# Experts over lists of token rows, in blocks of 128 with register-addressed weights, in place of every expert over every token

## The reference

```python
x = x + attention(layernorm(x), ctx)          # 16 heads, causal, gate, Wo
xf = layernorm(x)
scores = softmax(xf @ gate_w)                 # 8 experts
top_scores, top_idx = top_k(scores, 2)
scale = zeros((T, E)).at[arange(T)[:, None], top_idx].set(top_scores)
xs = scale.T[:, :, None] * xf[None]           # an expert that was not chosen sees zeros
h = silu(einsum('etd,edh->eth', xs, w1)) * einsum('etd,edh->eth', xs, w3)
x = x + einsum('eth,ehd->etd', h, w2).sum(0)
```

## Time and profile before

| | |
|---|---|
| median of 3 runs | 680.01 us (677.1 to 682.3) |
| span of the profiled execution | 676.9 us |
| TensorE busy | 644.6 us, 95% |
| VectorE, ScalarE, GpSimd busy | 471.3, 379.5, 230.4 us |
| instructions | 13559 |

### The profile page before, as it was taken

One profiled execution on the slowest core, in us unless ns is written; L12 is line 12 of the kernel. 1 busy time (PEld: TensorE's weight loads), 2 busy tenths in 40 slices (PEclk: granted clock), 3 DMA queues, 4 the chain that ended last, 5 costly groups with the idle time before them and its releaser, 6 DMA issues.

```text
span 676.9 us, 13559 instructions
## 1 busy us (share of the span) xinstructions
PE 644.6 (95%) x5320; PEld 393.0 (58%) x5320; DVE 471.3 (70%) x981; ACT 379.5 (56%) x778; POOL 230.4 (34%) x283
## 2 busy tenths in 40 slices
PE   7887999999999999999999999999999999979997
PEld 3363565555565545554565556455456766768885
DVE  6637779998989999999989987412205533676454
ACT  2221456766646676667646677877784565123332
POOL 5005212522123115021005033385434434536662
PEclk9878799999999999999999899999999999999999
DMA  6985982010260000010093010102101021104100
GB/s 170 234 133 115 138 144 31 2 22 24 69 68 1 3 1 3 1 65 2 14 161 109 2 34 3 35 2 78 32 32 32 17 63 49 31 16 109 48 32 31
DMA packets 29305, 36.58 MB, mean 54 GB/s; under 512 B 5833, under 2 KB 16457, under 8 KB 29242
## 3 DMA queue, kind: packets, MB, share of 16 engines
q1 hardware_dynamic: 26248, 34.53, 24.6%
q10 hardware_dynamic: 946, 0.92, 0.4%
q0 software_dynamic: 2048, 0.27, 0.3%
HBM read 25.58 MB, written 8.06 MB: 50 GB/s over the span
## 4 chain that ended last, share of the span: by engine, by line
PE 45%; DVE 12%; ACT 3%; POOL 2%; issue 1%; DVEq 0%; ACTq 0%; POOLq 0%
PE bank L1600 9%; DVE pmax L1303 9%; PE bank L1578 8%; PE bank L1664 4%; PE bank L1666 4%; PE bank L1665 4%; PE bank L1429 3%; PE bank L1545 3%; PE bank L1685 2%; PE bank L1686 2%; ACT probs L1160 2%; PE bank L1688 2%; DVE xn_sb L1274 1%; PE bank L1610 1%; PE bank L1583 1%
## 5 line engine op out<-in xcount | busy, mean ns | idle before, releaser
L1160 ACT ACTIVATE probs<-bank 128x512 f32<-128x512 f32 (+4 forms) x592 | 283.2, 555 | 147.0 <-PE bank L1578 87.5
L1303 DVE TENSOR_REDUCE pmax<-bank 128x1 f32<-128x512 f32 (+6 forms) x640 | 322.7, 574 | 29.4 <-PE bank L1549 15.9
L1578 PE MATMUL bank<-qaug,kaug 64*128 64x512 f32 (+4 forms) x592 | 151.6, 455 | 2.5 <-DVE pmax L1303 1.1
L1600 PE MATMUL bank<-probs,vaug 128*32 128x256 f32 (+4 forms) x2048 | 142.3, 390 | 2.2 <-ACT probs L1160 1.8
L1545 PE MATMUL bank<-kaug,qaug 62*128 62x512 f32 (+6 forms) x640 | 135.0, 404 | 9.8 <-DVE stage L807 3.4
L1578 PEld LDWEIGHTS bank<-qaug,kaug 64*128 64x128 f32 (+1 forms) x592 | 66.2, 183 | 85.7 <-ACT probs L1160 29.8
L1545 PEld LDWEIGHTS bank<-kaug,qaug 62*128 62x128 f32 x640 | 76.5, 189 | 40.7 <-DVE pmax L1303 21.0
L1600 PEld LDWEIGHTS bank<-probs,vaug 128*32 128x32 f32 (+1 forms) x2048 | 52.3, 109 | 53.3 <-ACT probs L1160 18.4
L1032 POOL TENSOR_TENSOR h_lo<-v_sb,h_hi 128x512 fp32r<-128x512 f32 x31 | 40.1, 1295 | 66.3 <-ACT h_hi L1216 66.3
L1396 DVE SCALAR_TENSOR_TENSOR v_sb<-t_sb,v_sb 128x512 f32<-128x512 f32 x32 | 24.2, 757 | 45.2 <-POOL v_sb L1028 38.2
L1216 ACT ACTIVATE h_hi<-v_sb 128x512 fp32r<-128x512 f32 x32 | 20.4, 637 | 57.4 <-DVE v_sb L1396 55.5
(11 more groups left out here) (143 smaller groups left out, 824.4 us busy)
## 6 DMA issues: line engine op xcount, KB each, us to landing
qaug<-s_dram SPq DMA_DIRECT2D x32, 256.0 KB, 3.4
qaug<-q_parts SPq DMA_DIRECT2D x18, 256.0 KB, 9.2
q_parts<-stage SPq DMA_DIRECT2D x7, 512.0 KB, 2.9
k_parts<-stage SPq DMA_DIRECT2D x4, 512.0 KB, 5.0
w_sb<-in_w SPq DMA_DIRECT2D x4, 512.0 KB, 10.0
out<-x_sb SPq DMA_DIRECT2D x8, 256.0 KB, 2.3
ctx_sb<-in_ctx_t SPq DMA_DIRECT2D x3, 512.0 KB, 6.4
x_sb<-in_x SPq DMA_DIRECT2D x3, 512.0 KB, 6.3
```

Of the source, the lines that this page charges most:

```text
L1160: act.activation(probs[0:rows, u % NSLOT, h, off:CH], bank_of(e)[0:rows, off:CH], ACT.Exp, scale=DK ** -0.5).then_inc(act_read, 1)
L1303: dve.tensor_reduce(pmax[:, n % 2, qt, h, slot:slot + 1], bank[:, 0:w], AX_X, ALU.max).then_inc(dve_read, 1)
L1578: last.append(pe.matmul(pair[side][0][0:r, off:CH], keys_at(b, ROWS, hp, P * j, r), qaug[b:b + ROWS, p % 2, hp, off:CH], start=True, stop= ...
L1600: last = pe.matmul(psum[O_BANK][32 * h:32 * h + 32, q0:q1], vaug[0:r, col:col + 32], probs[0:r, u % NSLOT, h, q0:q1], start=(j == 0), stop ...
```

## The change

The feed's 32 dense steps go. In their place each token's row (scaled by its score) is written once for each of its two experts into a list in DRAM, and the lists are worked off in blocks of 128 rows. The lists are made twice: chunks 1, 2 and 3 together (`SETS[0]`), which give at most 24 blocks filled and 7 more for parts of blocks, 31, and chunk 0 (`SETS[1]`), which gives 15: 46 blocks, always run, empty ones on zeros. After `rank` of a chunk, `cnt` counts on TensorE and VectorE the rows ahead of each token and gives its two places (`slots`), `wide` makes the two scaled rows (GpSimd for chunks 1 and 2, VectorE for 3 and 0), and `scat` sends them by 8 indirect transfers from GpSimd's queue. After a set's last chunk, `tail` writes zeros behind each list (9 transfers by SP, 8 of them with an address that SP loads into a register), and `table` computes on VectorE which expert and which place each block has, and where each token's two results will lie.

A block i is then: `bl` (SP loads a register, then the rows), `bx` (2 transposes; ScalarE `row_hi`, VectorE `row_lo`), `bab` (6 products of 256 columns, w1 and w3 side by side; tanh on ScalarE, two VectorE instructions), `bh` (1 transpose; `h_hi`, `h_lo`), `by` (3 products of 256 columns, copied by ScalarE) and `bst` (SP stores 128 KB). The rows are now the stationary operand and the weights the moving one, at an address from a register that TensorE loads for each block. `back` fetches each token's two results by indirect transfers (4 for 256 tokens, in GpSimd's queue), `add` adds them and `out` stores.

```diff
-Y_BANKS = (5, 6)
+SETS = ((1, 2, 3), (0,))
+LAGS = {"bx": 0, "bab": 1, "bh": 2, "by": 3}
+RING = 3
+SET_OF = {c: s for s, chunks in enumerate(SETS) for c in chunks}
+ROOM = tuple(TPC * len(chunks) + 1 for chunks in SETS)
+COUNT = tuple(2 * TPC * len(chunks) + E - 1 for chunks in SETS)
+BLOCKS = [(s, b) for s, count in enumerate(COUNT) for b in range(count)]
+LAST_BLOCK = tuple(sum(COUNT[:s + 1]) - 1 for s in range(len(SETS)))
...
+XIN, YOUT, GOT = 4, 3, 3
+W_STEP = 3 * D
...
+            ("rank", c), ("cnt", c), ("wide", c), ("scat", c)] + ([("tail", SET_OF[c]), ("table", SET_OF[c])] if c == SETS[SET_OF[c]][-1] else [])
...
+def block_steps():
+
+    steps, count = [], len(BLOCKS)
+    for i in range(count + max(LAGS.values())):
+        for kind, lag in LAGS.items():
+            if 0 <= i - lag < count:
+                steps.append((kind, i - lag))
     return steps
```

The transfers of SP and GpSimd:

```diff
+                elif kind == "tail":
+
+                    s = e[1]
+                    sp.wait_ge(tail_ready, s + 1)
+                    sp.wait_ge(none_set, 1)
+                    sp.dma_start(sent[s][E * ROOM[s], :, :], none_sb[:, :]).then_inc(tail_out[s], 16)
+                    for ex in range(E):
+                        at = sp.value_load(tail_at[0:1, s, ex:ex + 1], min_val=0, max_val=P * E * ROOM[s] - P)
+                        sp.dma_start(sent[s].rearrange("r p d -> (r p) d")[bass.ds(at, P), :], none_sb[:, :]).then_inc(tail_out[s], 16)
+                elif kind == "bl":
+
+                    i = e[1]
+                    s, b = BLOCKS[i]
+                    if b == 0:
+                        sp.wait_ge(table_ready, s + 1)
+                        sp.wait_ge(tail_out[s], 16 * (E + 1))
+                        for c in SETS[s]:
+                            sp.wait_ge(scattered[c], 16 * 2 * TPC)
+                    if i == 0:
+                        sp.wait_ge(*made(last_st[last_unit[G * (NC - 1) - 1]]))
+                    if i >= XIN:
+                        sp.wait_ge(*taken(("bx", i - XIN)))
+                    at = sp.value_load(read_i[0:1, s, b:b + 1], min_val=0, max_val=E * ROOM[s])
+                    sp.dma_start(row_in[:, i % XIN, :], sent[s][bass.ds(at, 1), :, :].rearrange("r p d -> (r p) d")).then_inc(row_landed[i % XIN], 16)
+                elif kind == "bst":
+
+                    i = e[1]
+                    s, b = BLOCKS[i]
+                    sp.wait_ge(*taken(("by", i)))
...
+                elif kind == "scat":
+
+                    c = e[1]
+                    s = SET_OF[c]
+                    pool.wait_ge(slots_ready, POS[c] + 1)
+                    to = sent[s].rearrange("r p d -> (r p) d")
+                    for t in range(TPC):
+                        for k in range(2):
+                            pool.wait_ge(rows_wide, 2 * TPC * POS[c] + 2 * t + k + 1)
+                            pool.indirect_dma_start(to, bass.IndirectOffsetOnAxis(ap=slots[:, c, k, t:t + 1], axis=0), wide(k, t), None
+                                                    ).then_inc(scattered[c], 16)
+                elif kind == "back":
+
+                    _, c, part = e
+                    s, g = SET_OF[c], got_at[(c, part)]
+                    for r in range(YOUT):
+                        pool.wait_ge(y_stored[r], 16 * sum(1 for i in range(LAST_BLOCK[s] + 1) if i % YOUT == r))
+                    if g >= GOT:
+                        pool.wait_ge(added, g - GOT + 1)
+                    if g == 0:
+                        for o in ORDER[0:NC - 1]:
+                            pool.wait_ge(*made(("logits", o)))
+                    pool.wait_ge(back_ready, s + 1)
+                    rows = fed[s].rearrange("r p d -> (r p) d")
+                    for k in range(2):
+                        for t in range(2):
+                            pool.indirect_dma_start(got[:, g % GOT, k, t, :], None, rows,
+                                                    bass.IndirectOffsetOnAxis(ap=back_at[:, k, 2 * g + t:2 * g + t + 1], axis=0)
```

ScalarE and VectorE (`step` is an instruction that the next one waits for):

```diff
+                elif kind == "bh":
+                    i = e[1]
+                    act.wait_ge(*made(e))
+                    if i >= RING:
+                        act.wait_ge(*made(("by", i - RING)))
+                    act.activation(h_hi[:, i % RING, :], bank_of(e)[:, 0:P], ACT.Copy).then_inc(h_hi_ready, 1)
+                elif kind == "by":
+                    i = e[1]
+                    act.wait_ge(*made(e))
+                    if i >= YOUT:
+                        act.wait_ge(y_stored[i % YOUT], 16 * (i // YOUT))
+                    act.activation(y_sb[:, i % YOUT, :], bank_of(e)[:, 0:D], ACT.Copy).then_inc(act_read, 1)
...
+                elif kind == "bab":
+                    i = e[1]
+                    if i >= RING:
+                        dve.wait_ge(*made(("bh", i - RING)))
+                    dve.wait_ge(tanh_done, i + 1)
+                    step(dve.scalar_tensor_tensor(out=at_sb[:, i % RING, :], in0=t_sb[:, i % RING, :], scalar=1.0, in1=bank[:, 0:HID],
+                                                  op0=ALU.add, op1=ALU.mult))
+                    dve.scalar_tensor_tensor(out=h_sb[:, i % RING, :], in0=at_sb[:, i % RING, :], scalar=0.5, in1=bank[:, HID:2 * HID],
                                              op0=ALU.mult, op1=ALU.mult).then_inc(dve_read, 1)
...
+                elif kind == "bh":
+                    i = e[1]
+                    dve.wait_ge(h_hi_ready, i + 1)
+                    if i >= RING:
+                        dve.wait_ge(*made(("by", i - RING)))
+                    dve.tensor_tensor(h_lo[:, i % RING, :], bank[:, 0:P], h_hi[:, i % RING, :].bitcast(F32), ALU.subtract).then_inc(dve_read, 1)
+                elif kind == "add":
                     _, c, part = e
-                    t0 = TPC * c + 2 * part
+                    g, t0 = got_at[(c, part)], TPC * c + 2 * part
                     view = x_sb[:, t0:t0 + 2, :]
-                    dve.tensor_tensor(view, bank[:, :].rearrange("p (t d) -> p t d", t=2), view, ALU.add).then_inc(dve_read, 1)
+                    dve.wait_ge(got_landed[g % GOT], 64 * (g // GOT + 1))
+                    step(dve.tensor_tensor(view, got[:, g % GOT, 0, :, :], view, ALU.add))
+                    dve.tensor_tensor(view, got[:, g % GOT, 1, :, :], view, ALU.add).then_inc(added, 1)
 
 
```

TensorE:

```diff
+                elif kind == "bx":
+                    i = e[1]
+                    pe.wait_ge(row_landed[i % XIN], 16 * (i // XIN + 1))
                     bank = make(e)
                     for a in range(KD):
-                        hi, lo = (w[:, ex, part, HID * a:HID * (a + 1)] for w in (w_hi, w_lo))
-                        x_high, x_low = x_hi[POS[c] % 2][:, a, :], x_lo[:, c, CH * a:CH * (a + 1)]
-                        pe.matmul(bank[:, :], hi, x_high, start=(a == 0), stop=False)
-                        pe.matmul(bank[:, :], hi, x_low, start=False, stop=False)
-                        last = pe.matmul(bank[:, :], lo, x_high, start=False, stop=(a == KD - 1))
+                        last = pe.transpose(bank[:, P * a:P * (a + 1)], row_in[:, i % XIN, P * a:P * (a + 1)], ident[:, :])
                     last.then_inc(dve_full, 1)
-                elif kind == "y":
-                    _, c, ex = e
-                    i = feed_at[(c, ex)]
+                    s, b = BLOCKS[i]
+                    if b == 0:
+                        pe.wait_ge(table_ready, s + 1)
+                    whose[i] = pe.value_load(whose_i[0:1, s, b:b + 1], min_val=0, max_val=E - 1)
...
+                        high, low = (row[:, i % 2, P * a:P * (a + 1)] for row in (row_hi, row_lo))
+                        hi, lo = (w[:, bass.ds(whose[i] * W_STEP + D * a, D)] for w in w_all)
+                        pe.matmul(bank[:, 0:D], high, hi, start=(a == 0), stop=False)
+                        pe.matmul(bank[:, 0:D], low, hi, start=False, stop=False)
+                        last = pe.matmul(bank[:, 0:D], high, lo, start=False, stop=(a == KD - 1))
+                    last.then_inc(dve_full, 1)
+                elif kind == "bh":
+                    i = e[1]
+                    pe.wait_ge(*taken(("bab", i)))
                     bank = make(e)
...
+                    pe.transpose(bank[:, 0:P], h_sb[:, i % RING, :], ident[:, :]).then_inc(dve_full, 1)
+                elif kind == "by":
+                    i = e[1]
+                    pe.wait_ge(*taken(("bh", i)))
+                    bank = make(e)
+                    hi, lo = (w[:, bass.ds(whose[i] * W_STEP + KD * D, D)] for w in w_all)
+                    pe.matmul(bank[:, 0:D], h_hi[:, i % RING, :], hi, start=True, stop=False)
+                    pe.matmul(bank[:, 0:D], h_lo[:, i % RING, :], hi, start=False, stop=False)
+                    pe.matmul(bank[:, 0:D], h_hi[:, i % RING, :], lo, start=False, stop=True).then_inc(act_full, 1)
```

550 lines of the change are left out of this document (286 added, 264 removed).

## The result

The changed kernel takes 675.36 us (median of 20 runs, from 672.39 up) against 680.25 us for the kernel before; the ratio is 0.9937 with a 95% interval of 0.9921 to 0.9953. It is 0.6% faster: the interval leaves out 1, but the gain is under the 1% that the prediction counts as no change. The forecast of 690 us, slower, was wrong. One of the 20 runs, a slow one of 2618.75 us, is left out of the ratio. The profiled execution took 673.26 us with a span of 671.5.

What follows compares the result with a forecast made beforehand. The prediction took TensorE's work, mostly the feed, to bound the kernel after 445 us. Start of blocks 541 + blocks 115 + router 13 + end 18 = 687 us of span, 690 us as median; range 648 to 735 us.

Steps and rivals of the forecast that it cites:

- 46 x 2.5 = 115 us: All 46 blocks on TensorE: a period of 2.5 us each, 115 us in sum, bounds 71 and 145.
- the 0.95 us taken for register load and register instructions together: TensorE in each block: register load plus eight register instructions cost 0.95 us on top of 1.55 us for 12 instructions.
- The 5 us more at the maxima: Attention up to 436 us: counting for chunks 1 and 2 on busy VectorE among the maxima adds 5 us.
- Last exponentials: End of the attention: last exponential at 525 us as a sign, attention ending at 527 us in the working.
- First block: Start of the blocks after chunk 3's router, lists and transfers: 541 us, ends 533 to 556.
- An indirect transfer: GpSimd's queue: one indirect transfer of 128 rows takes 1.1 us, possibly up to 2.2 us.
- Chunk 0's router among the blocks: VectorE's router and list work for chunk 0, some 23 us, adds 13 us among the blocks; ends 0 and 24.
- The end: After the last by: copy, store, eight indirect transfers, two additions, final store; 18 us, against about 5 before.
- The 24 transfers of the first set, 26 us on GpSimd, fit beside the 15 blocks: GpSimd during the second set's blocks: the first set's 24 transfers, 26 us, fit beside 15 blocks of 37 us.
- (1): Blocks on TensorE: register load hides in the queue, period 1.75 us, 650 us span, 653 us median; chance 0.27.
- (2): Blocks on TensorE: clock falls to the 1.2 GHz level, 41 us more, 731 us; chance 0.13.
- (3): GpSimd's queue: indirect transfers take 2.2 us each, 37 us more, 727 us; chance 0.15.

Runs made afterwards that it cites:

- e_const: Changed kernel with the first expert's weights at a fixed address for all blocks and no register load on TensorE (wrong outputs); 671.2 us, ratio 0.9885.
- e_place: Changed kernel with block i+1's register load moved behind block i's six first-layer products; 673.69 us, ratio 0.9914.
- e_unused: Changed kernel with each block's register still loaded but unused, the first expert's weights at a fixed address (wrong outputs); 670.06 us, ratio 0.9871.
- e_zero: Changed kernel with the second list's rows zeroed early by one transfer, its nine tail transfers dropped; 671.55 us, ratio 0.9875.
- e_spread: e_comb with chunk 0's table instructions in nine pieces among successive blocks and its eight row scalings on GpSimd; 666.59 us, ratio 0.979.
- e_comb: Changed kernel with output stores last in SyncE's order, additions planned later and the second list zeroed early; 669.64 us, ratio 0.9848.
- e_gather: Changed kernel with every second gather left out and the first result added twice (outputs incomplete); 665.5 us, ratio 0.9762.
- e_back: Changed kernel with the planner's back cost raised from 4400 to 8000, so additions and output transfers stand later; 672.5 us, ratio 0.9868.
- e_two: Changed kernel with each block loading its register twice in a row, the first unused; 692.23 us, ratio 1.0214.

## Why the prediction was wrong

**The step that failed** is "46 x 2.5 = 115 us", in it the 0.95 us taken for register load and register instructions together. Measured are 0.48 us, and a period of 1.93 us where 2.5 was put: 46 x 0.57 = 26 us too much. The 1.55 us for the 12 instructions were nearly right (1.45 in `e_const`). The bounds were fair (0 to 1.6), and the value was taken above the middle because eight register instructions come on top. `e_place` shows that these cost nothing where no load stands just ahead of them, and `e_unused` that an unused load costs 0.12; the whole price stands right behind the load, and it is half of what was taken. The text's own break-even of 2.28 us and its "wrong if the period is under 2.1" name the same quantity.

**The other terms held.** The 5 us more at the maxima came out as 3 (the last 159 exponentials begin at 438.4 us, at 435.4 before). Last exponentials: 525 predicted as a sign (527 in the working), 525.8 measured. First block: 541 and 539.6. An indirect transfer: 1.1 and 1.25 us, of which 0.95 are work. Chunk 0's router among the blocks: 13 us, and 41.1 - 15 x 1.93 = 12.1 us in the first 15 distances, of which `e_zero` shows 4.0 to be SyncE's hold by `tail` and `e_spread` another 3 VectorE's table and row scalings (37.5 us there in `e_comb`, 34.5 in `e_spread`). The end: 18 and 21.0 us; of the 3 us 1.2 are in the gathers and 2.4 in the time from the last product to the first gather (5.2 us for 2.8), of which `e_gather` saves 2.7; the last store took less than was put.

**Two terms were missing.** "The 24 transfers of the first set, 26 us on GpSimd, fit beside the 15 blocks" is true of GpSimd (620.0 to 650.8 us), but the prediction didn't ask what stands behind the additions in VectorE's and SyncE's orders. From 580.7 us to the last row's transposes (643.2) the blocks need 62.5 us, where 30 x 1.93 is 57.9: 4.6 us; with later additions they need 59.4 (`e_back`). And a block passes through four stages: from the last row's transposes to the last product it is 7.25 us, of which the product 46 x period counts only one period, so 5.3 are missing.

**The sum, by its terms.** 687 (span) - 1.4 (start) - 26.2 (period) - 0.9 (router) + 4.6 (stall) + 5.3 (last block's stages) + 3.0 (end) = 671.4 us, against 671.5 measured. This closes by its making, since the terms cut the measured span into pieces; what it shows is which piece was off and by how much. The bounding engine and the list of costs were right, the likeliest case's one large term was mis-sized by half, and two small ones were left out.

**The rivals.** (1), the load hides, had 0.27 and a time of 653 us. It is partly what happened: the price is half of what was put. But the 653 us would not have come even with all of it hidden, since `e_const` without any load takes 671.2. What bounds it then, the additions in VectorE's order and GpSimd's 32 gathers behind the first list's last block, stood in no rival. (2), the clock, fell as stated: from 584 to 620 us the granted clock is 1.00. It is 0.92 and 0.94 in the stretches beside it; the products ran at 1.2 GHz behind the 3.31 us wait shown above, and again at about 578 and 636 us, where TensorE had just stood idle for 2.13 and 1.55 us. By the granted clock some 10 us of the 76 in these two stretches were at the lower level, so an estimate of its price is 5 us at most, and it sits inside the router's 12 us and the 4.6 us of stall. The Trainium skill (TensorE: Matmul & The Clock Gate, "HAM oscillation — how this bites in real kernels") says that bursts with waits between them bring the clock down again and again. It shows this for waits that are longer than the bursts. Here the gap is the shorter part, 0.48 us of 1.93, so the prediction was wrong to say that by that rule this is the case, and the clock of 1.00 does not speak against the rule. (3), transfers at 2.2 us, fell by 1.25 measured, though it named the right queue. A second load right behind the first measures 0.63 us here (`e_two`). The figure that the Trainium skill gives for a tensor load, some 600 ns (DMA: Bandwidth & Descriptors, "Latency and other measured facts"), agrees with this. As the price in a block the measured 0.48 us is lower; the period by that figure, 2.15 us, would have been 0.22 too long.

**Where the expected gain went.** The feed's 140 us on TensorE became 46 x 1.45 = 67 us, 73 less. Against that stand about 14 us from the last exponentials to the first block, in which TensorE has little, 12 of chunk 0's router among the blocks, 22 of registers (46 x 0.48), 5 of stall behind 580 us and 16 more at the end than before (21.0 for about 5): 69 us. Each of the large ones but the first was changed by a run of its own. The count is rough: it leaves out 3 us at the maxima and 5.3 of the last block's stages, and counts in full a router that the kernel before had too. That it leaves 4 us, about what was measured, is luck.

## What to carry to other kernels

Once work with few long products is replaced by many short steps, ask each in-order queue what stands behind each wait: here additions that wait for gathers in front of a block's `h_lo`, nine transfers of zeros in one piece in front of row loads, and an 18-instruction table on the engine that every block needs. When a block gets cheaper and the time does not follow, look for the queue whose work starts only when a whole list is done (GpSimd's 32 gathers of 1.3 us): only what brings that start forward, or what is left of it behind the last block, counts. How often a list is made is a trade of its own: in this kernel both one list and an earlier first list lost to the split that hides most gathers.
